# Inverse square roots of query and key variances: one power on GpSimd in place of eleven Newton operations of VectorE

## What is computed

```
def _layernorm(t, gamma, beta):
    mu = jnp.mean(t, axis=-1, keepdims=True)
    var = jnp.var(t, axis=-1, keepdims=True)
    return (t - mu) * jax.lax.rsqrt(var + LN_EPS) * gamma + beta
q = (x @ Wq.T + bq).reshape(B, N, H, D).transpose(0, 2, 1, 3)
kv = (y @ Wkv.T + bkv).reshape(B, M, 2, H, D).transpose(2, 0, 3, 1, 4)
k, v = (kv[0], kv[1])
q = _layernorm(q, q_gamma, q_beta) * SCALE
k = _layernorm(k, k_gamma, k_beta)
attn = jax.nn.softmax(jnp.einsum('bhnd,bhmd->bhnm', q, k), axis=-1)
```

## Time and profile before

| | before |
|---|---|
| median of 3 runs | 1395.9 us (1394.43 to 1395.96) |
| the profiled execution's own time | 1382.54 us |
| its span, first to last instruction | 1380.7 us |
| PE busy | 1240.6 us (90%) |
| DVE busy | 984.4 us (71%) |
| ACT busy | 698.1 us (51%) |
| POOL busy | 450.4 us (33%) |
| chain that ended last, share of PE | 82% |

### The profile page before, as it was taken

One profiled execution on the slowest core, in us unless ns is written; L12 is line 12 of the kernel. 1 busy time (PEld: TensorE's weight loads), 2 busy tenths in 40 slices (PEclk: granted clock), 3 DMA queues, 4 the chain that ended last, 5 costly groups with the idle time before them and its releaser, 6 DMA issues.

```text
span 1380.7 us, 54869 instructions
## 1 busy us (share of the span) xinstructions
PE 1240.6 (90%) x22808; PEld 1024.0 (74%) x22808; DVE 984.4 (71%) x2498; ACT 698.1 (51%) x1377; POOL 450.4 (33%) x436
## 2 busy tenths in 40 slices
PE   3789999999999999999999999999999986699950
PEld 3677878888888878788878787888888864488840
DVE  7458777777777777777777777777777763365547
ACT  1345555555555555555555555555555542255520
POOL 1322333333333333333333333333333222155530
PEclk7789999999999999999999999999999998699985
DMA  4100111111111111103111100111111002586558
GB/s 155 39 21 4 48 49 49 49 49 49 49 49 51 56 44 51 34 30 100 33 34 33 36 29 28 34 33 34 34 38 33 15 14 63 157 245 188 163 188 262
DMA packets 82579, 92.12 MB, mean 67 GB/s; under 512 B 17248, under 2 KB 72544, under 8 KB 82016
## 3 DMA queue, kind: packets, MB, share of 16 engines
q1 hardware_dynamic: 70816, 65.41, 16.4%
q0 software_dynamic: 6912, 19.01, 3.8%
q10 hardware_dynamic: 4608, 4.20, 0.9%
HBM read 61.19 MB, written 33.78 MB: 69 GB/s over the span
## 4 chain that ended last, share of the span: by engine, by line
PE 82%; DVE 9%; issue 4%; DMA 2%; ACT 1%; POOL 1%; SPq 0%; DVEq 0%; POOLq 0%; ACTq 0%
PE ringB L489 16%; PE ringC L500 14%; PE oA L582 10%; PE banksS L565 9%; DVE mx L1220 6%; PE banksS L783 5%; PE banksS L529 4%; PE ringB L663 3%; PE ringB L617 2%; PE ringB L649 2%; PE banksS L634 2%; PE ringB L484 2%; DMA out<-ksq 2%; PE oA L489 2%; PE banksS L544 2%
## 5 line engine op out<-in xcount | busy, mean ns | idle before, releaser
L863 ACT ACTIVATE pt<-banksS 128x1024 f32<-128x1024 f32 x128 | 127.7, 1023 | 129.6 <-PE banksS L565 118.0
L1039 POOL TENSOR_TENSOR kn<-kc,rr 128x512 f32<-128x512 f32 x64 | 66.6, 1062 | 336.0 <-DVE rr L1208 336.0
L500 PE MATMUL ringC<-wx_kv,ct 128*128 128x256 f32 x512 | 159.9, 312 | 13.6 <-DVE ws_down L1362 6.2
L1220 DVE TENSOR_REDUCE mx<-banksS 128x8 f32<-128x2048 f32 x64 | 146.3, 2287 | 0.9 <-PE banksS L544 0.9
L500 PE MATMUL ringC<-wx_kv_rest,ct 128*128 128x256 f32 x512 | 146.8, 287 | 0.0
L500 PE MATMUL ringC<-wx_kv,ct_rest 128*128 128x256 f32 x512 | 146.0, 285 | 0.0
L1033 POOL TENSOR_TENSOR sc<-sc,rz 128x1024 f32<-128x1024 f32 x32 | 62.3, 1948 | 223.5 <-DVE rz L1281 223.5
L565 PE MATMUL banksS<-qT,kT 17*128 17x64 f32 x4096 | 132.4, 278 | 0.9 <-DVE qT L1225 0.9
L565 PEld LDWEIGHTS banksS<-qT,kT 17*128 17x128 f32 x4096 | 123.5, 191 | 7.9 <-issue 1.4
L500 PEld LDWEIGHTS ringC<-wx_kv,ct 128*128 128x128 f32 x512 | 99.3, 194 | 27.6 <-DVE pos_u L1338 7.8
L1234 DVE RECIPROCAL rz<-oA 128x128 f32<-128x128 f32 x64 | 61.3, 957 | 55.5 <-PE oA L582 55.5
(11 more groups left out here) (219 smaller groups left out, 2957.0 us busy)
## 6 DMA issues: line engine op xcount, KB each, us to landing
ct_in<-in_ctxT SPq DMA_DIRECT2D x64, 256.0 KB, 3.1
pt<-rows_by_expert SPq DMA_DIRECT2D x80, 130.0 KB, 2.4
rows_by_expert<-in_pad_rows SPq DMA_DIRECT2D x16, 260.0 KB
xt<-in_x SPq DMA_DIRECT2D x32, 128.0 KB, 3.5
rows_without_experts<-base SPq DMA_DIRECT2D x32, 128.0 KB
pt<-expert_rows SPq DMA_DIRECT2D x16, 256.0 KB, 4.1
kn<-expert_rows SPq DMA_DIRECT2D x16, 256.0 KB, 4.2
out<-ksq ACTq DMA_DIRECT2D x32, 128.0 KB, 3.8
```

The costliest lines, as they stand in the source:

```text
L500: mm = pe.matmul(ringC[:, half * DIM:(half + 1) * DIM], left[:, p, k, j // 2, (j % 2) * P:(j % 2 + 1) * P], right[:, k, part * DIM:(part + ...
L863: act.activation(pt[:, g, :, :, :, :].rearrange("p i q c n -> p i (q c n)"), banksS[:, :, g * 256:(g + 1) * 256], ACT.Exp)\
L1039: pool.tensor_tensor(kn[:, 2 * jj:2 * jj + 2, :, 0:HD].rearrange("p j h d -> p (j h) d"), kc[:, 2 * jj:2 * jj + 2, :].rearrange("p j (h d) ...
L1220: dve.tensor_reduce(mx[:, 2 * r:2 * r + 2, :, HD].rearrange("p q i -> p i q"), banksS[:, :, :].rearrange("p i (q m) -> p i q m", q=2), AX. ...
```

## The change

The power moves to POOL. DVE keeps the sums and the mean squares plus epsilon (now `mean_squares`). POOL gets a new part `inverse_sigmas` in its list at lag 2, right ahead of `keys_scaled`: one `tensor_tensor` of `ss` (128x80) to the power of `minushalf` (a column of -0.5, read again for each of the 80), into `rr`. `nt` goes. DVE's sums wait until the power of the tile before has read `ss`, the power waits until the queries of the tile before have read `rr`, and both scalings wait for the power. The semaphores of the power and of the two key scalings are now one, counted three per tile.

```
--- before.py
+++ after.py
@@ -143,7 +143,6 @@
         head_ones = sb("head_ones", [P, 2, 2 * HD])
         ss = sb("ss", [P, 5 * H])
         rr = sb("rr", [P, 5 * H])
-        nt = sb("nt", [P, 5 * H])
         qn = sb("qn", [P, H, PAD])
         kn = sb("kn", [P, 4, H, PAD])
         wx_kv_in = kc[:, :, :].rearrange("p (k a) n -> p k (a n)", k=KD)
@@ -283,8 +282,8 @@
         ev = {}
         for ln in "abc":
             ev.update(chain(f"{ln}_norm", f"{ln}_stats", f"{ln}_meanvar", f"{ln}_veps"))
-        ev.update(chain("newton", "s_eps", "s_shift", "newton_y0", *(f"newton_{s}" for n in range(3)
-                        for s in (f"t{n}", f"u{n}", f"y{n + 1}"))))
+        ev.update(chain("s_eps", "s_eps"))
+        ev.update(chain("sigmas", "sigmas_ready", "kn1_ready", "kn0_ready"))
         ev.update(chain("weights_b0", "weights0", "weights1"))
         ev.update(chain("weights_b1", "weights2", "weights3"))
         ev.update(chain("rz", "rz0", "rz1"))
...
@@ -1033,8 +1032,13 @@
                 pool.tensor_tensor(pn[:, :, :], ex[:, :, :], rz2[:, :].unsqueeze(2).to_broadcast([P, 2 * HP, N]),
                                    ALU.mult).then_inc(ev["pn_ready"].sem, 1)
 
+            def inverse_sigmas(c, p):
+                pool.wait_ge(ev["s_eps"].sem, ev["s_eps"].of(c))
+                freed(pool, ev["qn_ready"], c)
+                pool.tensor_tensor(rr[:, :], ss[:, :], minushalf[:, :].to_broadcast([P, 5 * H]), ALU.pow).then_inc(ev["sigmas_ready"].sem, 1)
+
             def keys_scaled(c, p, jj):
-                pool.wait_ge(ev["newton_y3"].sem, ev["newton_y3"].of(c))
+                pool.wait_ge(ev["sigmas_ready"].sem, ev["sigmas_ready"].of(c))
                 freed(pool, full["KT"], c)
                 pool.tensor_tensor(kn[:, 2 * jj:2 * jj + 2, :, 0:HD].rearrange("p j h d -> p (j h) d"),
                                    kc[:, 2 * jj:2 * jj + 2, :].rearrange("p j (h d) -> p (j h) d", d=HD),
@@ -1058,6 +1062,7 @@
                 on(s, odd, 2, cross_rstd)
                 on(s, odd, 5, ffn_rstd)
                 on(s, odd, 4, self_biased)
+                on(s, odd, 2, inverse_sigmas)
                 on(s, odd, 2, keys_scaled, 1)
                 on(s, odd, 2, keys_scaled, 0)
                 on(s, odd, 6, rows_scattered, 1)
@@ -1172,6 +1177,7 @@
 
             def key_sums(c, p, jj):
                 dve.wait_ge(ev[f"k_sq{jj}"].sem, ev[f"k_sq{jj}"].of(c))
+                freed(dve, ev["sigmas_ready"], c)
                 dve.tensor_reduce(ss[:, H * (1 + 2 * jj):H * (3 + 2 * jj)],
                                   ksq[:, 2 * jj:2 * jj + 2, :].rearrange("p j (h d) -> p (j h) d", d=HD), AX.X, ALU.add)\
                     .then_inc(ev[f"k_sum{jj}"].sem, 1)
@@ -1182,33 +1188,18 @@
                 dve.tensor_tensor(qc[:, :], ringC[:, 0:DIM], rows[:, 0, :], ALU.add).then_inc(free["Q"].sem, 1)
 
             def query_sums(c, p):
+                freed(dve, ev["sigmas_ready"], c)
                 dve.wait_ge(ev["q_sq"].sem, ev["q_sq"].of(c))
                 dve.tensor_reduce(ss[:, 0:H], qsq[:, :].rearrange("p (h d) -> p h d", d=HD), AX.X, ALU.add).then_inc(ev["q_sum"].sem, 1)
 
-            def inverse_sigmas(a, p):
+            def mean_squares(a, p):
 
                 for s in ("q_sum", "k_sum0", "k_sum1"):
                     dve.wait_ge(ev[s].sem, ev[s].of(a))
                 dve.tensor_scalar(ss[:, :], ss[:, :], 1.0 / HD, EPS, ALU.mult, ALU.add).then_inc(ev["s_eps"].sem, 1)
-                dve.wait_ge(ev["s_eps"].sem, ev["s_eps"].of(a))
-                dve.tensor_scalar(nt[:, :].bitcast(I32), ss[:, :].bitcast(I32), 1, None, ALU.arith_shift_right)\
-                    .then_inc(ev["s_shift"].sem, 1)
-                dve.wait_ge(ev["s_shift"].sem, ev["s_shift"].of(a))
-                for jj in range(2):
-                    freed(dve, ev[f"kn{jj}_ready"], a)
-                freed(dve, ev["qn_ready"], a)
-                dve.tensor_scalar(rr[:, :].bitcast(I32), nt[:, :].bitcast(I32), -1.0, MAGIC, ALU.mult, ALU.add)\
-                    .then_inc(ev["newton_y0"].sem, 1)
-                for n in range(3):
-                    dve.wait_ge(ev[f"newton_y{n}"].sem, ev[f"newton_y{n}"].of(a))
-                    dve.scalar_tensor_tensor(nt[:, :], rr[:, :], -0.5, rr[:, :], ALU.mult, ALU.mult).then_inc(ev[f"newton_t{n}"].sem, 1)
-                    dve.wait_ge(ev[f"newton_t{n}"].sem, ev[f"newton_t{n}"].of(a))
-                    dve.tensor_tensor(nt[:, :], nt[:, :], ss[:, :], ALU.mult).then_inc(ev[f"newton_u{n}"].sem, 1)
-                    dve.wait_ge(ev[f"newton_u{n}"].sem, ev[f"newton_u{n}"].of(a))
-                    dve.scalar_tensor_tensor(rr[:, :], nt[:, :], 1.5, rr[:, :], ALU.add, ALU.mult).then_inc(ev[f"newton_y{n + 1}"].sem, 1)
 
             def queries_scaled(c, p):
-                dve.wait_ge(ev["newton_y3"].sem, ev["newton_y3"].of(c))
+                dve.wait_ge(ev["sigmas_ready"].sem, ev["sigmas_ready"].of(c))
                 freed(dve, full["QT"], c)
                 dve.tensor_tensor(qn[:, :, 0:HD], qc[:, :].rearrange("p (h d) -> p h d", d=HD),
                                   rr[:, 0:H].unsqueeze(2).to_broadcast([P, H, HD]), ALU.mult).then_inc(ev["qn_ready"].sem, 1)
@@ -1375,7 +1366,7 @@
                 on(s, odd, 2, key_sums, 0)
                 on(s, odd, 2, query_sums)
                 on(s, odd, 5, routing_logits)
-                on(s, odd, 2, inverse_sigmas)
+                on(s, odd, 2, mean_squares)
                 if s == TILES - 1 + 5:
                     on(s, odd, 5, two_best)
                     on(s, odd, 5, rows_placed)
```

More of the change, by code:

```diff
@@ L297, in perceiver_block @@
             ev[f"scattered{p}"] = Event(scattered[p], 32 - 16 * p, 16)
-        for n in ("a_rstd b_rstd c_rstd k_sq0 k_sq1 k_sum0 k_sum1 kn0_ready kn1_ready pv0 pv1 pv2 pv3"
+        for n in ("a_rstd b_rstd c_rstd k_sq0 k_sq1 k_sum0 k_sum1 pv0 pv1 pv2 pv3"
                   " ct_ready ct_rest_ready xn_ready xres_ready q_sq q_sum qn_ready shift_ready x1n_ready x1b_ready tanh_ready mx2_ready ex_ready"
```

7 lines of the change are left out of this document (4 added, 3 removed).

## The result

The kernel is **slower by 12.7%**: 1574.2 us median of 4 runs (1566.85 to 1574.61) against 1395.2 us median of 4 runs (1393.14 to 1395.96) of the kernel before on the same chip; ratio 1.127, 95% interval 1.125 to 1.129. That is 179 us more, where the prediction had 72. The time lies inside the range given, and the direction was right.

The account below looks back on a forecast made before the run. PE, busy 90% of the span, was taken to bound the kernel. 67 us of stalls over 29 steps plus 5 us in the first tile gave 72 us over 1395.9 us, so 1468 us; range 1393 to 1640 us.

Parts of the forecast that it names:

- I cost its removal at nothing: Newton operations on DVE: removing 83 us of DVE time over 32 tiles was taken to save no time.
- the size of P: P is the time of the new 128x80 power on POOL ahead of the key scaling, put at 8.0 us.
- the 0.37: Microseconds by which a one-column power exceeds a one-column multiply; a quarter of it was charged for each further column.
- The choice between 0.7 and 30 us: Ends for the power's time: further columns at a multiply's rate, or each costing the full 0.37 us again.
- the power is far longer, P over 13 us: Rival: the power's columns follow one another with no overlap, 732 us more, up to 2130 us; chance 0.14.
- `hot` stands still while POOL's two-input instructions run: DVE's `hot` pair beside POOL's power: for P over 3.2 us it waits, leaving DVE free at 611.98 + P.
- the chip doesn't let the power block `hot`: Rival: DVE's `hot` runs beside the power, so only the first tile loses 5 us, 1401 us; chance 0.05.
- the direct one, 9.4 us: Longest power on POOL that still leaves the keys scaled when PE wants them at 622.17.
- the recorded path: Power delays `hot`, then `rz` and `oT`; PE stalls before the weighted values for P - 5.7 us, 29 times.
- the clock, left at nothing: Stalls might slow TensorE's clock, at worst 4 us a tile, 116 us in all; none was counted in the forecast.
- the three signs of being wrong: Power's mean under 5.7 us, `hot` running through while the power does, or the clock falling in the steady part.
- a wait for `oT`: Expected new PE wait before the weighted values for DVE's `oT`, about 2.3 us, 29 times.

Follow-up runs that it names:

- Experiment 3: Kernel before, all Newton operations kept, plus an 80-column power of ones on POOL ahead of the key scalings, result unread: 1564.55 us, ratio 1.1237.
- experiment 2: Kernel before without its eleven Newton operations, scaling by mean squares: 1399.97 us, ratio 1.0055; control keeping them plus a copy of the mean squares: 1384.85 us.
- the ladder: Kernel before plus one unread POOL power (1 to 80 columns) or multiply in each of steps 6 to 33: 1390.74 us, one execution.
- experiment 4: Changed kernel with 32 idle identity transposes on PE from tile 3 on, while it would wait for keys: 1536.05 us, ratio 1.1011 to the kernel before.

## Where the prediction was right and where wrong

- **Right: what bounds the kernel, and that DVE's relief is worth nothing.** Experiment 3 loses 172 us with all Newton operations in place, and experiment 2 gains nothing without them. "I cost its removal at nothing" was even friendly: in experiment 2 the scatter that moved with the keys costs some 13 us.
- **The first failed step is the size of P**: "I take a quarter of it, 0.095 us a column: P = 0.55 + 7.5 = 8.0 us". A column costs 0.159 us, 43% of the 0.37, and P is 13.13. The choice between 0.7 and 30 us was said to be one; a ladder of column counts would have settled it, and a single row of one column could not split start from column. At 13.13 us P lies just inside the rival "the power is far longer, P over 13 us" (0.14), whose reason, columns with no overlap, fits the straight line of the ladder; its price of up to 732 us took the whole 0.37 us for a column.
- **The second is the path**: "`hot` stands still while POOL's two-input instructions run". That held for multiplies and was carried over to the power. The power doesn't hold DVE: `hot` 231 ns, Newton operations 242 ns inside it. The rival "the chip doesn't let the power block `hot`" was given 0.05, and it is what happens. With it the limit is the direct one, 9.4 us, worked out in the prediction, and it measured true: 13.1 - 9.4 = 3.7 us a step, against 83.1 us in 22 waits, 3.8 each, between 160 and 1080 us. The wait stands before the turned keys, not before the weighted values.
- **The two errors partly cancelled, which is luck.** By the recorded path and the real P the sum would be 29 x (13.1 - 5.7) + 10 = 225 us; by the direct path and P = 8.0 it would be 5 us. The 72 us came from a limit 3.7 us too low, set against a P 5.1 us too low. That the time lies in the range and the direction is right doesn't speak for the working: the stall that it forecast never came.
- **The third is the clock, left at nothing.** The loop's waits and the first tile's 13.8 - 3.6 = 10.2 give 120.7 us (124.3 - 3.6). Of the other 58 us to 179, experiment 4 gives back 38 by keeping the clock up, and explains part of the rest by the wait for `x1n` that a faster PE meets. In the profiled executions the sum closes: 192.1 us are 112.9 of idle time and 79.2 by which the same instructions ran longer. The text had 0 to 116 us for it and took the end; its own showed both levels, and where the clock had held, PE had been idle for 1.2 us in all, a third of the wait of 3.8.
- **Signs.** Two of the three signs of being wrong came: `hot` ran through beside the power, and the clock fell in the steady part. Seen as told: DVE down by 81 us, the power's row 32 times. Not seen: 8 us for it (13.1), POOL up by 256 us (420), `hot` at 6 us (0.37 for the pair), a wait for `oT`. The first wait for keys, foretold as 8.6 us, is 13.8, as the same working gives with the real P: 3.57 + 13.13 - 3.04 = 13.7.
